# A two-stage residual LoRA kernel on one core: order of sums, parts and loads around the down projection's first and last blocks, LoRA A of the leftover tiles in 128 rows, and t's repeated rows on VectorE

## What is computed

```python
def _L0_cond_ref(x, W_gate, W_up, W_down, A_gate, B_gate, A_up, B_up, A_down, B_down, lora_indices, layer_idx):
    def lora_add(base, inp, A, B):
        Ab = A[layer_idx][lora_indices]
        Bb = B[layer_idx][lora_indices]
        t = jnp.einsum('bri,bni->bnr', Ab, inp)
        return base + jnp.einsum('bor,bnr->bno', Bb, t) * SCALE
    gate = lora_add(jnp.einsum('bnh,fh->bnf', x, W_gate), x, A_gate, B_gate)
    up = lora_add(jnp.einsum('bnh,fh->bnf', x, W_up), x, A_up, B_up)
    act = jax.nn.silu(gate) * up
    down = lora_add(jnp.einsum('bnf,hf->bnh', act, W_down), act, A_down, B_down)
    return down
...
x = x + _L0_cond_ref(x, ..., itok_B_2_6, 0)
x = x + _L1_cond_ref(x, ..., itok_B_1_7)   # x @ weight.T + bias + scale * (x @ A.T) @ B.T
```

## Time and profile before

| | |
|---|---|
| time, median of 3 (lowest, highest) | 1622.85 us (1622.76, 1622.96) |
| the profiled execution: time, span | 1623.45 us, 1621.7 us |
| PE busy | 1571.4 us (97%), 6820 matmuls |
| VectorE, ScalarE, GpSimd busy | 1058.7 us (65%), 602.2 us (37%), 967.0 us (60%) |
| mean granted TensorE clock | 0.989 |
| DMA | 189.02 MB, mean 117 GB/s |

### The profile page before, as it was taken

The page is one execution under the profiler, slowest core; times in us unless marked ns, Lnnn a source line. Parts: engine busy times, 40 slices in busy tenths (PEclk is TensorE's granted clock), DMA queues, the critical chain, the costliest instruction groups (busy, mean ns, idle before and its releaser), DMA issues.

```text
span 1621.7 us, 20870 instructions
## 1 busy us (share of the span) xinstructions
PE 1571.4 (97%) x6820; PEld 1281.6 (79%) x6820; DVE 1058.7 (65%) x1045; ACT 602.2 (37%) x1043; POOL 967.0 (60%) x679
## 2 busy tenths in 40 slices
PE   6999999999999999999999998999999999899998
PEld 4778888888887788888888776888788886778886
DVE  5786666677777866666677655564747448855433
ACT  3744444444446444444444332222222314331110
POOL 5477767767774877777666775666665742631110
PEclk9999999999999999999999999999999999999999
DMA  8334544533544355345552664534344340203322
GB/s 159 101 108 127 166 120 127 166 101 101 152 114 108 110 165 167 114 127 166 127 127 75 229 181 110 131 110 118 110 122 119 108 132 23 57 17 81 80 52 54
DMA packets 290798, 189.02 MB, mean 117 GB/s; under 512 B 164676, under 2 KB 252740, under 8 KB 290372
## 3 DMA queue, kind: packets, MB, share of 16 engines
q1 hardware_dynamic: 229344, 123.70, 30.5%
q10 hardware_dynamic: 61220, 63.98, 11.9%
q0 software_dynamic: 128, 0.00, 0.0%
HBM read 132.55 MB, written 56.46 MB: 117 GB/s over the span
## 4 chain that ended last, share of the span: by engine, by line
PE 81%; SPq 5%; issue 4%; DVE 3%; DMA 2%; POOL 2%; ACT 2%; ACTq 0%; DVEq 0%; POOLq 0%
PE ps L2417 81%; SPq L603 1%; SPq L1472 1%; SPq L1437 1%; ACT Bf L1780 1%; DMA act_scratch<-c21buf 1%; DMA raw<-in_L_cond_B_down_dram 1%; POOL moving L2293 0%; DMA turned_w<-in_L_cond_W_down_dram 0%; SPq L1429 0%; SPq L1401 0%; SPq L1454 0%; POOL Bf L2285 0%; DMA raw<-in_L_cond_W_up_dram 0%; DVE tw_down L1140 0%
## 5 line engine op out<-in xcount | busy, mean ns | idle before, releaser
L2417 PE MATMUL ps<-X_T,W 128*128 128x512 f32 x1944 | 460.8, 392 | 5.5 <-POOL W L2203 3.8
L2417 PEld LDWEIGHTS ps<-X_T,W 128*128 128x128 f32 x1944 | 368.1, 189 | 83.7 <-issue 6.7
L2417 PE MATMUL ps<-X_B,W 128*128 128x512 f32 x1728 | 417.6, 391 | 14.2 <-ACT X_B L1708 13.0
L2417 PEld LDWEIGHTS ps<-X_B,W 128*128 128x128 f32 x1728 | 325.6, 189 | 83.8 <-issue 14.4
L2203 POOL TENSOR_TENSOR W<-s,W 128x512 fp32r<-128x512 f32 x156 | 229.0, 1476 | 55.1 <-ACT W L1679 52.3
L2293 POOL TENSOR_TENSOR moving<-landed,moving 128x1024 fp32r<-128x1024 f32 x70 | 173.0, 2480 | 131.0 <-ACT moving L1933 130.9
L1101 DVE TENSOR_TENSOR acc<-acc,ps 128x1024 f32<-128x1024 f32 x140 | 167.7, 1212 | 112.5 <-PE ps L2417 112.3
L2417 PE MATMUL ps<-moving,Ws_S 128*128 128x512 f32 x960 | 225.3, 395 | 11.6 <-issue 7.4
L2417 PEld LDWEIGHTS ps<-moving,Ws_S 128*128 128x128 f32 x960 | 183.1, 191 | 52.3 <-issue 8.2
L2203 POOL TENSOR_TENSOR W<-TG,W 128x512 fp32r<-128x512 f32 x88 | 124.2, 1412 | 122.7 <-ACT W L1679 122.3
L1679 ACT ACTIVATE W<-s 128x512 fp32r<-128x512 f32 x156 | 98.2, 632 | 221.9 <-PE ps L2417 202.4
(11 more groups left out here) (167 smaller groups left out, 1944.4 us busy)
## 6 DMA issues: line engine op xcount, KB each, us to landing
raw<-in_L_cond_W_gate_dram SPq DMA_DIRECT2D x164, 128.0 KB, 3.0
raw<-in_L_cond_W_up_dram SPq DMA_DIRECT2D x164, 128.0 KB, 3.2
landed<-moves_scratch SPq DMA_DIRECT2D x40, 512.0 KB, 4.6
moves_scratch<-t_move ACTq DMA_DIRECT2D x60, 256.0 KB, 3.6
landed<-act_scratch SPq DMA_DIRECT2D x30, 512.0 KB, 5.2
raw<-in_x_dram SPq DMA_DIRECT2D x104, 128.0 KB, 3.2
act_scratch<-c21buf ACTq DMA_DIRECT2D x42, 256.0 KB, 2.4
turned_w<-in_L_cond_W_down_dram SPq DMA_DIRECT2D x80, 128.0 KB, 3.4
```

The costliest lines, as they stand in the source:

```text
L2417: return nc.tensor.matmul(dst, stationary, moving, start=start, stop=stop, skip_group_check=True)
```

## The change

In six parts:

1. `t_high`, `t_low`: the rows of `Tm` that repeat the high part are made by VectorE (a copy of `Tm`'s own rows) instead of ScalarE, four copies in each half.
2. `third_unit`: S2 of the next unit is split ahead of `Bf`, on ScalarE and on GpSimd.
3. The last unit of the second half: the last three differences T3, T2, T4 go from GpSimd to VectorE (`last_moves`); sums S3 stand ahead of the half tile's product, sums S2 and the first turned LoRA A of down behind it; S2's high part is made ahead of the last unit's end; `load_acc` is issued in another order, one of them some places later.
4. The start of down: S4, S3, A12 and A22 follow one step earlier; SP loads LoRA A (`load_ad`) earlier, and the pieces 7 and 8 between the weights of the next block.
5. The leftover tiles: their LoRA A stands in a wider `Ad` (zeros included), so that the parts of two pairs fill 128 rows; the part of pr = 1 is summed in the same PSUM tile as the last `seven_t`, and the part of pr = 0 in one `tacc` with it. The 12 matmuls stay 12. Their activations are rounded and split after step P7 instead of between steps, pr = 1 first, and the half tile's low part goes from VectorE to GpSimd (its rows are loaded twice).
6. The last block: PSUM pairs are taken in the order 0, 1, 2, 3; `td_mask` goes, the mask being the scale of `td_copy` on ScalarE and of one scalar_tensor_tensor of 32x256 on VectorE; `td_low` and `bd_low` change places.

```diff
@@ t_low
                 eng.wait_ge(t_hi, h * 4 + 2 * p + w + 1)
+                V.tensor_copy(Tm[w][TM_AGAIN[w], cols], Tm[w][rows, cols].bitcast(F32))
@@ last_unit
+                if h == 1:
+                    last_moves(U - 1)
...
-                    half_tile_first(U)
-                    for j in range(2):
-                        sum_weights(0, "S3", j)
+                    for j in range(2):
+                        sum_weights(0, "S3", j)
+                    half_tile_first(U)
+                    for j in range(2):
+                        sum_weights(0, "S2", j)
+                    turn_ad(0)
                 half_tile_second(U)
+            def last_moves(U):
+
+                n = pair_number(U)
+                wait_moved(eng, n, "T1")
+                eng.wait_ge(act1_done, U + 1)
+                eng.wait_ge(act2_done, U + 1)
+                V.tensor_tensor(keep[:, :], vbuf[:, :], keep[:, :], ALU.subtract).then_inc(moves_last.up((n, "T3")), 1)
...
@@ td_first
-                    V.tensor_tensor(tw_down[:, cols], tw_down[:, cols], tacc[rows, pr, :], ALU.add
-                                    ).then_inc(td_before, 1)
+                    for b in range(2):
+                        first = pr * T + p * TT + b * NS
+                        one = tw_down[:, first:first + NS]
+                        last = V.scalar_tensor_tensor(out=one, in0=tacc[rows, pr, b * NS:(b + 1) * NS],
+                                                      scalar=t_mask[rows, b:b + 1], in1=one, op0=ALU.mult,
+                                                      op1=ALU.add)
+                    last.then_inc(td_masked, 1)
@@ load_sevens
-                some(0, 5)
+                some(0, 2)
                 load_ad(0)
+                some(3, 5)
                 load_ad(1)
-                some(6, 8)
+                load_moving(6)
                 for p in (2, 3):
                     for e in range(2):
                         load_down(("D", p, e))
+                    load_moving(p + 5)
                 some(9, 12)
@@ ScalarE, third_unit
                 w_high(U + 1, "A11")
+                w_high(U + 1, "S2")
                 b_high(U + 1)
-                w_high(U + 1, "S2")
@@ ScalarE, sevens_block
                         elif n == 2:
-                            full_high(0)
                             ad_high(LAST)
-                        elif n == 3:
-                            full_high(1)
                         elif n == 4:
-                            last_high(0)
-                            last_high(1)
+                            for pr in (1, 0):
+                                full_high(pr)
+                                last_high(pr)
@@ seven_t on TensorE
+                if event == LAST_T:
+                    last = t_last(dst, 1, False)
                 last.then_inc(pe_s.up(event), 1)
```

More of the change, by code:

```diff
@@ L584, in b_rounded, with wait_moved @@
             return b_round[rows, 0:2 * HC].rearrange("p (r f) -> p r f", r=2)
+        def wait_moved(eng, n, m):
+            order = moves_last if (n, m) in moves_last.value else moves
+            eng.wait_ge(order.sem, order.after((n, m)))
         def moves_stored(eng, pairs):
@@ L1559, in load_last @@
                 sp.wait_ge(pe_s.sem, pe_s.after((SEVENS - 1, 1, "P3", 1)))
-                sp.dma_start(last_landed[:, :], act_d[FULL, 0:HC, :]).then_inc(last_loaded, 16)
+                for half in range(2):
+                    sp.dma_start(last_landed[half * HC:(half + 1) * HC, :], act_d[FULL, 0:HC, :]
+                                 ).then_inc(last_loaded, 16)
             def load_sevens():
@@ L1971, in sevens_block @@
                         if tp == 0:
-                            if b == 0 and n < 5:
-                                weights_both(0, ("S2", "S4", "S3", "A12", "A22")[n])
+                            if b == 0 and n < 4:
+                                weights_both(0, ("S4", "S3", "A12", "A22")[n])
                             elif b > 0 and n == 0:
@@ L2038, in ad_high @@
                 if p == LAST:
-                    A.activation(Ad[:, :, :, 0, :], Ad_turned[p % 2][:, :, :, :], ACT.Copy).then_inc(ad_hi, 1)
+                    eng.wait_ge(bf_lo, ALL)
+                    for c in range(2):
+                        A.activation(Ad[:, c, 0:3:2, :, :], zeros[:, :, :].rearrange("p j (l r) -> p j l r", l=2),
+                                     ACT.Copy)
+                    for src, home in last_ad_places(0):
+                        last = A.activation(home, src, ACT.Copy)
+                    last.then_inc(ad_hi, 1)
                     return
@@ L2057, in td_copy @@
                 for p in range(2):
-                    cols = slice(pr * T + p * TT, pr * T + (p + 1) * TT)
                     rows = slice((1 - p) * 2 * Q + Q, (2 - p) * 2 * Q)
-                    A.activation(tw_down[:, cols], tacc[rows, pr, :], ACT.Copy).then_inc(td_copied, 1)
+                    for b in range(2):
+                        first = pr * T + p * TT + b * NS
+                        last = A.activation(tw_down[:, first:first + NS], tacc[rows, pr, b * NS:(b + 1) * NS],
+                                            ACT.Copy, scale=t_mask[rows, b:b + 1])
+                    last.then_inc(td_copied, 1)
             def td_high(pr):
@@ L2314, in sevens_block @@
                         if tp == 0:
-                            if b == 0 and n < 5:
-                                weights_low(0, ("S2", "S4", "S3", "A12", "A22")[n])
+                            if b == 0 and n < 4:
+                                weights_low(0, ("S4", "S3", "A12", "A22")[n])
                             elif b > 0 and n == 0:
```

182 lines of the change are left out of this document (89 added, 93 removed).

## The result

The changed kernel took 1602.4 us (median of four, 1601.35 to 1603.35). Its ratio to the kernel before is 0.9884, with a 95% interval of 0.9871 to 0.9898. Run again beside the experiments it took 1602.25 us (five, 1598.24 to 1603.8), with a ratio of 0.9881 (0.9860 to 0.9902). It is faster by 18 to 20 us, where 26.5 were forecast. 1602 is inside the range and 6 us above the forecast.

A forecast was written before the change was run, and what follows sets the result against it. TensorE, busy 97% of the span, was taken as the bound. Gains of 4.8 + 1.7 + 10 + 4.5 + 5.5 = 26.5 us from the median 1622.85 gave 1596 us, range 1588 to 1606.

The forecast's parts named there:

- The places: The five parts of the kernel where TensorE's waits were to go; all giving most of 26.5 us had chance 0.70.
- t's repeated rows: At `Bf` in both halves: ScalarE loses four operations, so TensorE's waits go; 4.8 us (4.0 to 5.0).
- the term of `b_low`: For `Bf`: `b_low` would run from 57.8 instead of 60.33 and end near 59.3, before TensorE needs it at 60.07.
- the drop behind the wait: Behind the 1.81 us wait for `Bf` in half 0: a lower clock costing 1.6 us would go too.
- S2 ahead of `Bf`: Third unit, both halves: a 1.4 to 1.9 us wait for S1 replaces S2's 1.88; gain 1.7 us (0 to 4).
- End of the second half and SyncE's queue: Around down's start: the 3.86 us wait goes and P6 starts earlier despite waits for pieces 7 and 8; 10 us (7 to 12).
- the start of S4: Down's first block: GpSimd works without a pause from S4 at 931 on, so A22 is ready at 950.8.
- GpSimd is held up by VectorE: Rival, end of half 1: five operations put A22 at 954 instead of 950.8; 1599 to 1600 us, chance 0.12.
- SP's queue gives the gain back: Rival, down's first block: pieces 7 and 8 come late behind weights, P6 starts near 984; 1602 us, chance 0.09.
- Down's last steps: Leftover tiles: piece 68 split once landed, so P2's wait of 3.04 and drop of 1.8 go; 4.5 us (3.5 to 5).
- The last block: Masks no longer hold up additions; waits of 1.7 us without a drop replace 4.3 and 2.9 of clock; 5.5 us (2.5 to 7.5).
- The clock: Behind TensorE's long waits: the granted clock falls to its lower level, priced at 1.6 to 2.9 us each.

The follow-up runs named there:

- the experiment: The changed kernel with t's repeated rows written by ScalarE again: 1603.04 us, ratio 0.9897 to the kernel before, against 0.9881 for the changed kernel.

## Why the prediction was right, and where it was off

**The places** were right: each wait that the forecast removed is gone or small in the trace. The sign and the range held. The sum was 6 to 8 us too large.

**t's repeated rows**, 4.8: about 2.6 by the experiment. Mis-sized were the term of `b_low` (1.50, it took 3.01 beside VectorE, so it ends 1.1 us earlier in each half and not 2.6) and the drop behind the wait (1.6, certain in the text, absent in the experiment and in before's second profile). VectorE's copy took 0.42, not 0.7.

**S2 ahead of `Bf`**, 1.7: wait for S1 of 1.2 (1.4 to 1.9 said), no drop behind it, and 0.6 for `vbuf`, which the forecast missed, as it named nothing behind the later sums on VectorE. By the traces it is worth about 2 us, by the times nothing that can be told.

**End of the second half and SyncE's queue**, 10 (7 to 12): measured 4.8, below its range. Here the forecast failed. I had "The wait goes: 3.86 + 2.4" and priced S4's sums ahead of the first addition at 0 to 1.4, in effect at nothing. P6 waits 2.75 in both profiles. VectorE's timeline in the changed kernel:

```profile
908.95 1.57 DVE L1037 TENSOR_TENSOR keep<-vbuf,keep 128x512 f32<-128x512 f32 x1
910.44 2.88 DVE L1039 TENSOR_TENSOR t_move<-vbuf,t_move 128x512 f32<-128x512 f32 x1
...
914.95 4.58 DVE L1081 TENSOR_TENSOR turned_w<-turned_w 128x512 f32<-128x512 f32 x2
...
924.62 3.48 DVE L1081 TENSOR_TENSOR w_sum<-turned_w,w_sum 128x512 f32<-128x512 f32 x2
928.13 4.61 DVE L1131 TENSOR_TENSOR acc<-acc,ps 128x1024 f32<-128x1024 f32 x4
```

The sums ended at 928.1, and only then came the addition that frees P6's tile, which TensorE wanted at 926.8. That they are the cause was shown by moving them (0.31 left). But this alone gave nothing, because the next link was as late: S4's high part behind ScalarE's five loads, which the forecast left out. It had GpSimd work without a pause "from S4 at 931 on", 11.1 us behind the start of P1 (919.88), and A22 at 950.8, 30.9 behind it. In both profiles of the changed kernel S4 began 16.8 and A22 ended 34.8 us behind P1 (its 950.5 only looks like the forecast's 950.8, since P1 itself began 4.2 us earlier, at 915.7). With the loads moved, S4 began 12.5 and A22 ended 30.5 behind P1. So the step that failed is the start of S4: the loads ahead of it were priced at nothing, where they make A22 3.9 us late, and its own sums at nothing, where they cost P6 2.75. The forecast itself says that all behind A22 is late with it, and 10 less 3.9 is 6.1, where the two first profiles differ by 6.2; in the changed kernel's second, P5' waited 2.78 with a drop behind it, and 3.9 are left. With the loads moved and SyncE's order mended the stretch gives 11.1 us, and with the sums moved too 14.5, where the change gives 4.8. P1' waited 2.3 to 2.4 of the 3.2 forecast, and P5' 0.3 or 2.8 of "1.8 or less". That the queue's new order is a gain at all is likely (1.6 to 5.3 us by the traces, within the uncertainty of the times); the forecast didn't see that piece 7 could have gone ahead of the weights for 4.9 more by the ratios.

**The rivals.** "GpSimd is held up by VectorE" had A22 3.2 us late. It was 3.9 late, but by ScalarE's loads: with these moved it came in time, and GpSimd had stood idle for 5.58 ahead of S4. The neighbour cost time elsewhere: on VectorE's own sums and on `b_low`. "SP's queue gives the gain back" had 1602 us and P6' at 984, 64.1 behind P1, by pieces that come late behind the weights. The measured time is that number, and P6' (24 matmuls behind the start of P5') came about 63 and 65 us behind P1 in the two profiles. But the cause isn't the rival's: from the start of the weights it took 15.1 us to P1' and 22.7 to P5' in the first profile (15.0 and 23.5 in the second), where the forecast had 15.1 and 22.4. The queue was priced right, and the weights themselves started 3.9 us late. So a time of 1602 doesn't speak for this rival.

**Down's last steps**, 4.5: 5.4. **The last block**, 5.5: 6.9, with waits of 1.3 for the forecast 1.7 and no drop. Of the cause I had half: masked additions took 1.86 to 2.22 us for four, but the plain masks cost 1.27 in this place. The other parts of these two terms (the half tile's split on GpSimd, t of the left-over tiles in 128 rows) weren't tried by themselves.

**The clock** was priced as fixed, some 11 us in all. It takes 1.7 us each time, but at waits of 1.9 to 2.8 it falls in one execution and not in another. The one profile of before had more drops than its second, and the reference was 2 us high. What stays open is which part of the spread of 5 us in one kernel's times is clock and which is waits that differ, as before's `Bf` does, or issues that do, as the five loads with 5.0 to 7.0 us.

## What to carry to other kernels

Where a wait has two or three causes of nearly equal date, removing one may show nothing, as here; list for the waiting matmul every chain with its date (here sums 928, loads on ScalarE 932, place of piece 7), each counted from one matmul that both kernels share and not from the start of the trace, and move them together. Put a transfer ahead of a long batch on its queue if its place comes free first. Price an operation by its neighbour at the new place, not by its row at the old one, and a clock drop by a chance.

## What was not expected of the hardware

The same wait drops the clock in one execution and not in the next: 2.75 us in six of nine profiles, 1.88 in four of six, 1.2 in none of 22. Operations on 128x512 with two operands in SBUF took on VectorE 0.64 to 2.88 us (two sums 1.28 alone and 4.58 beside GpSimd), and two splits of 32x256 on GpSimd 1.51 or 3.01, while the additions to `acc` with one operand in PSUM took 1.2 whatever ran beside them. Of eight transfers one took 4.6 us to issue when four loads of 1 MB had been queued by another engine 7 us before.
